# One block for an attention layer and a mixture of experts, with the experts' first operands made in the last attention chunks

## The reference

```python
# attention, per sequence of 512 tokens, 16 heads of 32
q, k, v = relu(x @ w_q.T), relu(x @ w_k.T), x @ w_v.T
vk  = einsum('bhen,bhdn->bhed', pad(v, one row of 1.0), k)
out = einsum('bhed,bhdn->bhen', vk, q)
out = out[:, :, :-1] / (out[:, :, -1:] + 1e-15)
x   = layernorm(x + out @ w_proj.T + b_proj)
# experts: 8, router by sigmoid of logits, golden zone, top-2 fallback
w    = router_weights(x @ Wr)
mid  = silu(x @ Wg[e] (+ LoRA)) * (x @ Wu[e] (+ LoRA))
x    = layernorm(x + sum_e w[:, e] * (mid @ Wd[e] (+ LoRA)))
```

## Time and profile before

| | us |
|---|---|
| median of 3 runs | 2446.73 |
| lowest and highest | 2446.03, 2448.91 |
| the profiled execution's own time | 2444.87 |
| its span | 2443.1 |
| mean granted TensorE clock, share of full | 0.976 |

### The profile page before, as it was taken

The page is one execution under the profiler, slowest core; times in us unless marked ns, Lnnn a source line. Parts: engine busy times, 40 slices in busy tenths (PEclk is TensorE's granted clock), DMA queues, the critical chain, the costliest instruction groups (busy, mean ns, idle before and its releaser), DMA issues. The chain is left out here.

```text
span 2443.1 us, 30851 instructions
## 1 busy us (share of the span) xinstructions
PE 2303.7 (94%) x10684; PEld 1868.2 (76%) x10684; DVE 1605.9 (66%) x2393; ACT 853.1 (35%) x1375; POOL 697.3 (29%) x499
## 2 busy tenths in 40 slices
PE   8897999999979999997999689999999999999997
PEld 6786788888857888885888468777777778888885
DVE  5556676777757956675344786667667886666665
ACT  4444222222214322222222254333344434444442
POOL 0002333444421222220000433224323543333331
PEclk9998999999989999998999999999999999999999
DMA  5654222222223001000000121222111121111110
GB/s 198 217 151 154 61 69 69 69 69 69 72 72 146 18 18 35 1 1 22 1 0 1 44 78 52 78 93 76 39 52 52 52 87 52 52 52 52 52 35 35
DMA packets 91010, 155.34 MB, mean 64 GB/s; under 512 B 6288, under 2 KB 55440, under 8 KB 84256
## 3 DMA queue, kind: packets, MB, share of 16 engines
q1 hardware_dynamic: 90912, 154.07, 18.8%
HBM read 114.20 MB, written 39.85 MB: 63 GB/s over the span
## 5 line engine op out<-in xcount | busy, mean ns | idle before, releaser
L1497 PE MATMUL moe_pu<-moe_b_hi,moe_a_hi 128*128 128x512 f32 x896 | 352.6, 394 | 25.3 <-ACT moe_c_last L1888 9.3
L1498 PE MATMUL moe_pu<-moe_b_lo,moe_a_hi 128*128 128x512 f32 x896 | 350.7, 391 | 0.0
L1499 PE MATMUL moe_pu<-moe_b_hi,moe_a_lo 128*128 128x512 f32 x896 | 350.5, 391 | 0.0
L2057 DVE TENSOR_TENSOR moe_a_lo<-moe_up_raw,moe_a_hi 128x512 fp32r<-128x512 f32 x192 | 185.6, 982 | 147.5 <-ACT moe_a_hi L1764 147.4
L1421 DVE SCALAR_TENSOR_TENSOR acc<-ffn_pd,ffn_wts,acc 128x512 f32<-128x512 f32 x256 | 177.8, 748 | 88.8 <-PE ffn_pd L101 88.6
L2089 DVE SCALAR_TENSOR_TENSOR acc<-moe_ring,moe_wts,acc 128x512 f32<-128x512 f32 x256 | 190.6, 746 | 63.0 <-PE moe_ring L1499 59.1
L1722 POOL TENSOR_TENSOR moe_h_lo<-moe_c_t,moe_h_hi 128x512 fp32r<-128x512 f32 x96 | 128.9, 1344 | 342.6 <-ACT moe_h_hi L1764 342.6
L1497 PEld LDWEIGHTS moe_pu<-moe_b_hi,moe_a_hi 128*128 128x128 f32 x896 | 169.4, 189 | 67.0 <-issue 24.5
L1497 PE MATMUL moe_ring<-moe_dn_hi,moe_h_hi 128*128 128x512 f32 x512 | 203.4, 397 | 6.4 <-DVE acc L2089 3.5
L1498 PE MATMUL moe_ring<-moe_dn_lo,moe_h_hi 128*128 128x512 f32 x512 | 200.2, 391 | 0.0
L1499 PE MATMUL moe_ring<-moe_dn_hi,moe_h_lo 128*128 128x512 f32 x512 | 199.9, 390 | 0.0
(11 more groups left out here) (403 smaller groups left out, 5263.5 us busy)
## 6 DMA issues: line engine op xcount, KB each, us to landing
moe_up_raw<-in_e_up SPq DMA_DIRECT2D x28, 1024.0 KB, 5.8
moe_dn_raw<-in_e_dn SPq DMA_DIRECT2D x28, 512.0 KB, 3.6
xh<-in_out_hi SPq DMA_DIRECT2D x32, 256.0 KB, 2.6
zs<-in_out_z SPq DMA_DIRECT2D x32, 256.0 KB, 3.2
xl<-in_out_lo SPq DMA_DIRECT2D x32, 256.0 KB, 3.4
ssd_z_raw<-zs SPq DMA_DIRECT2D x16, 512.0 KB, 3.9
in_w_raw<-in_in_w SPq DMA_DIRECT2D x4, 1024.0 KB, 7.7
x<-xh SPq DMA_DIRECT2D x8, 512.0 KB, 4.2
```

Source lines behind the costliest of these rows:

```text
L1497: pe.matmul(out, lh, rh, start=first, stop=False, skip_group_check=True)
L1498: pe.matmul(out, lh, rl, start=False, stop=False, skip_group_check=True)
L1499: return pe.matmul(out, ll, rh, start=False, stop=True, skip_group_check=True)
L2057: tt_(a_lo[:, q], src, raw(a_hi[:, q]), ALU.subtract).then_inc(s_alo, 1)
```

## The change

`attn_phase` is removed and its code moves into the experts' function, now `attn_experts`, with one set of semaphores and no barrier between the layers. Both layers' tiles are placed by hand; an operand of the experts that shares memory with an attention tile waits until that tile is read for the last time. The loops over sequences are written out as 16 chunks. PSUM tiles are shared: X is `pvk`, Y is (`pt`, `pk`), Z is `po`, the ring is (`pv`, `pq`).

- `xt` and ScalarE's copy into it are gone; TensorE transposes x from `acc`.
- GpSimd adds the bias to `acc` (`with_bias`, one 128x512 addition for each chunk), ahead of its part of the norm; VectorE's `norm_in` has one addition where it had two.
- In chunks 8 to 12 TensorE turns the eight chunks of the first half of the tokens (`ahead_x`), ScalarE copies them to `xr`. Chunk 12 makes the logits of parts, chunk 13 the plain logits and their turning.
- After chunks 8 to 11 ScalarE and VectorE cut the weights of q0 to q5 and x for q0 and q1. The first router's parts 0, 1, 2 stand after chunks 13, 14, 15, part 3 in the drain's first round; its comparison uses the second weight buffer as scratch, so the load of slot 1's weights waits for `s_router`.
- The drain's rounds 1 to 3 each make one product of slot 0 (`FIRST`) before `project`, and contain one `x_low` each; two more follow.
- Slot 0 now has the same lists as the others, without `down` and `add_down`.

The core of the diff:

```diff
+            def with_bias(n):
+                pool.wait_ge(s_xT, n + 1)
+                nc.gpsimd.tensor_tensor(acc[:, n], acc[:, n], bias[:], ALU.add).then_inc(s_xb, 1)
...
+            pool.wait_ge(s_bias, 16)
+            for n in range(NCH):
+                with_bias(n)
+                if n >= CPB and n != NCH - 1:
+                    deviation(n - CPB)
+                if n == 2 * CPB - 1:
+                    weight_sums(0, 0, 0, 0)
+                if n == 2 * CPB:
+                    weight_sums(0, 0, 0, 1)
+                    weight_sums(0, 0, 0, 2)
+                if n == PLAIN_AT:
+                    x_sums(0, 0)
+            deviation(NCH - CPB - 1)
             x_sums(0, 1)
+            deviation(NCH - CPB)
             x_sums(0, 2)
+            for m in range(NCH - CPB + 1, NCH):
+                deviation(m)
...
+        AHEAD = {8: (0, 1), 9: (2, 3), 10: (4, 5), 11: (6,), 12: (7,)}
+        PARTS_AT, PLAIN_AT, TOKENS_AT = 12, 13, 13
...
+            def ahead_x(i):
+                ch = sum(AHEAD.values(), ())[i]
+                if i:
+                    pe.wait_ge(s_xr, i)
+                pe.wait_ge(s_ln, ch + 2)
+                for kt in range(KT):
+                    ins = pe.transpose(pt[:, bass.ts(kt, P)], acc[:, ch, bass.ts(kt, P)], ident[:])
+                ins.then_inc(s_et, 1)
...
@@ ScalarE @@
+            for n in range(NCH):
+                chunk(n)
+                if n == 8:
+                    up_high(0, 0, 0, 0)
+                    up_high(0, 0, 0, 1)
...
+                if n == 13:
+                    router_functions(0, 0)
+                if n == 14:
+                    router_functions(0, 1)
...
@@ TensorE, drain round c @@
+                if c:
+                    ring.enter(0)
+                    up(0, *FIRST[c - 1])
+                pe.wait_ge(s_pa, m if c else m + 1)
+                project(m, (pv, pq)[c % 2])
@@ VectorE, after chunk n @@
+                if n == 13:
+                    dve.wait_ge(s_lgt, 1)
+                    router(0, 0)
+                if n == 14:
+                    router(0, 1)
+                if n == 15:
+                    router(0, 2)
+            for c in range(CPB):
+                m = NCH - CPB + c
+                divide(m)
+                if c:
+                    norm_out(m - 2)
+                low_out(m)
+                norm_in(m - 1, (pv, pq)[(c - 1) % 2] if c else pv)
+                if c == 0:
+                    router(0, 3)
+                if c < 3:
+                    x_low(0, (4, 2, 3)[c])
+            norm_out(NCH - 2)
+            x_low(0, 5)
+            norm_in(NCH - 1, (pv, pq)[(CPB - 1) % 2])
+            x_low(0, 6)
+            norm_out(NCH - 1)
```

More of the change, by code:

```diff
@@ L1830, in slot @@
                 more = not at(n, LAST)
-                plain = more and not at(n, 0, *MERGING)
+                plain = more and not at(n, *MERGING)
                 following = lambda *qs: [up_high(n + 1, 1 - s, u + s, q) for q in qs]
@@ new lines, in add_vk, with attend @@
+            def add_vk(n, c):
+                pe.wait_ge(s_vr, n + 1)
+                for g in range(G):
+                    bank = pvk[:, g // 2, (g % 2) * 256:(g % 2) * 256 + VW]
+                    ins = pe.matmul(bank, kk[:, bass.ts(g, P)], vo[:, g], start=(c == 0 and g % 2 == 0),
+                                    stop=(c == CPB - 1), skip_group_check=True)
+                ins.then_inc(s_vk, 1)
+            def attend(m):
+                pe.wait_ge(s_od, m + 1)
+                for g in range(G):
+                    ins = pe.matmul(po[:, g // 2, (g % 2) * 256:(g % 2) * 256 + OW], qT[:, m % CPB, g], bd[:, g],
+                                    start=True, stop=True)
+                ins.then_inc(s_o, 1)
@@ new lines, in turn_out, with project @@
+            def turn_out(m):
+                pe.wait_ge(s_od, m + 1 + 1)
+                for kt in range(KT):
+                    ins = pe.transpose(pk[:, bass.ts(kt, P)], o[:, kt].rearrange("p h d -> p (h d)"), ident[:])
+                ins.then_inc(s_oT, 1)
+            def project(m, bank):
+                pe.wait_ge(s_olo, m + 1 + 1)
+                for kt in range(KT):
+                    ins = product(pe, bank[:], (o_hi[:, kt], o_lo[:, kt]), (wp_hi[:, kt], wp_lo[:, kt]),
+                                  kt == 0, kt == KT - 1)
+                ins.then_inc(s_p, 1)
@@ new lines, in _ @@
+            turn_x(0)
+            for n in range(NCH):
+                chunk(n)
+            pe.wait_ge(s_bd, NB)
+            pe.wait_ge(s_qTc, NCH)
+            attend(NCH - CPB)
+            for c in range(CPB):
+                m = NCH - CPB + c
+                pe.wait_ge(s_olo, m + 1)
+                turn_out(m)
+                if c < CPB - 1:
+                    attend(m + 1)
+                if c:
[3 more added lines that the diff above has]
+                project(m, (pv, pq)[c % 2])
@@ new lines, in norm_out, with divide @@
+            def norm_out(m):
+                dve.wait_ge(s_arstd, m + 1)
+                ts(acc[:, m], rr[:], amv[:, 0:1], arstd[:], ALU.subtract, ALU.mult).then_inc(s_ln, 1)
+            def divide(m):
+                division.round(m)
+                dve.wait_ge(s_o, m + 1)
+                outs = po[:].rearrange("p t (g n) -> p (t g) n", g=2)
+                division.link(ts(den[:], outs[:, :, P:OW], AEPS, None, ALU.add))
+                division.link(nc.vector.reciprocal(den[:], den[:]))
+                dve.wait_ge(s_oT, m + 1)
+                for g in range(G):
+                    ins = tt_(o[:, g], outs[:, g, 0:P].rearrange("p (h d) -> p h d", h=HG),
+                              den[:, g].unsqueeze(2).broadcast_to([P, HG, AD]), ALU.mult)
+                ins.then_inc(s_od, 1)
@@ L2048, in _ @@
+            chain = Chain(dve, c_router, 0)
             link = chain.link
```

877 lines of the change are left out of this document (404 added, 473 removed).

## The result

| | us |
|---|---|
| median before, 11 runs | 2447.62 (2444.55 to 2448.99) |
| median after, 11 runs | 2441.82 (2438.55 to 2445.11) |
| ratio of the two, 95% interval | 0.9982 (0.9974 to 0.9990) |
| forecast | 2433, from 2422 to 2442 |

What follows compares the result with a forecast made beforehand. TensorE, busy 94% of the span, bounds the kernel, so only its standing time can be gained: -20.9 - 6.2 + 9.6 + 4.0 = -13.5 us, giving 2431.4 in the profile's terms and 2433 for the median, range 2422 to 2442.

Steps and rivals of the forecast that it cites:

- slot 1's -6.2: Slot 1: of 3.67 us idle time and 3.9 of low clock lost before, 1.4 remains, giving -6.2 us.
- TensorE's work moved into the chunks, +9.6: Chunks 8 to 13: turnings, plain logits, logits of parts and their turning cost full length, none hidden, +9.6 us.
- Waits in the chunks, +4.0: Chunks 11, 12, 14, 15: TensorE waits as GpSimd's additions hold up `norm_out` and router parts, taken as +4.0 us.
- The 5.3: Chunks 11, 12, 14, 15: sum of the waits if GpSimd always comes first, in full by the lock rule, 5.3 us.
- Table loads, 0: Chunks, ScalarE: table loads for sigmoid and exp lie in its idle time and cost nothing.
- The drain: After the last chunk: TensorE stands 5.9 us, rounds take 6.5, router part 3 4.9, turnings at T = 14.4, 20.9, 27.4.
- Slot 0: First expert slot: q4 starts at 43.1 after 4 us standing; slot 1 starts at T = 56.5, was 77.4: -20.9 us.
- (a): Chunks, drain, slot 0: waits don't come, the drain's 5.9 and slot 0's 4 us half filled; about 2424, chance 0.2.
- (b): Drain: longer, five `x_low` and norms held up by `x_sums`, gives back 8 to 10 us; about 2442, chance 0.17.
- (c): Chunks 8 to 15: lock rule in full strength makes `turn_out` wait; +22 us, 2455, slower; chance 0.08.
- (d): Slot 1's weights: their load waits for the router, so the change does not overlap; 2446, chance 0.03.

Runs made afterwards that it cites:

- g1: Changed kernel with 1248 bytes of its small tiles placed ahead of `xr`, bringing `a_lo` to 640 modulo 2048: 2429.71 us against 2446.13, 0.9933.
- h2: g1's kernel with router part 2 in chunk 15, part 3 before the drain's first division, early products one round earlier: 2425.95 us, 0.9911.
- e3: Kernel before with 32 bytes of padding before `a_lo` and 32 behind it: 2459.86 us, 1.0052.
- e4: Kernel before with 32 bytes of padding before `b_lo` and 32 behind it, every tile behind moving by 64 bytes: 2462.47 us, 1.0059.
- f3: Kernel before with pads of 64 bytes around `a_lo`: 2457.03 us, 1.0042.
- f4: Kernel before with pads of 64 bytes around `b_lo`: 2460.12 us, 1.0054.
- g2: Kernel before with 128 bytes ahead of `a_lo`, everything behind moving along: 2461.48 us, 1.0063.
- h4: Kernel before with both `b_hi` and `b_lo` 128 bytes off, `a_hi` and `a_lo` in step with the rest: 2460.54 us against 2445.76, 1.0056.
- e1: Changed kernel with 32 bytes of padding before `xr`, moving `xr`, raw up weights and `a_lo` to a multiple of 64: 2436.29 us against 2446.68, 0.9958.
- e2: Changed kernel with 32 bytes of padding behind the raw up weights, moving only `a_lo` and small tiles behind it: 2438.05 us, 0.9963.
- f1: Changed kernel with three small tiles (96 bytes) placed before `xr`, putting `a_lo` on a multiple of 128: 2435.56 us against 2445.81, 0.9958.
- h3: Kernel before with 128 bytes ahead of `h_hi` and `h_lo`, the down products' weights: 2452.69 us, 1.0029.

## Why the prediction was wrong

**The step that failed** is one that the sum leaves out: its last term is slot 1's -6.2, and the matmuls of all slots are taken at the pace that they had before. The change also placed every tile of the experts, and I put the new addresses at nothing without saying so; of the later slots the sum only says that written-out loops cost nothing. From slot 1 to the end of the span were 1021.3 us, the forecast makes it 1015.1, and 1028.7 were measured. With `a_lo` at the old distance modulo 256 (g1) they are 1014.9. So 13.8 us were lost there to 32 bytes, 12.1 by the medians of the two kernels. The slower groups alone make 17 of it (15 and 2); a part of that is taken back by shorter waits, which from slot 1 on are 16.4 us in all where g1 has 18.5.

With the bytes repaired the profiled execution is 13.3 us faster than the one before, and 13.5 were forecast; by the medians it is 16.4 (2429.7 where 2433 was forecast). That the first pair is so close is partly luck, since single executions of one kernel differ by more, and since two of the terms below miss in opposite directions.

Point by point, by its own steps:

- **TensorE's work moved into the chunks, +9.6**: the stretch shows +12.8, less 2.3 of waits, so 10.5. Right in mechanism, 0.9 too small. With the waits below, 1.7 too large, the two misses nearly cancel: 13.6 forecast, 12.8 measured.
- **Waits in the chunks, +4.0**: 2.3. The waits before the turnings in chunks 11 and 12 came at 0.69 and 0.68 (1.2 each forecast), the one at `turn_q` of chunk 14 at 0.96 (2.0), that of chunk 15 not at all (0.9). GpSimd was first, as the order of the lists said, but `norm_out` ended at t = 4.4, not 4.9 (1277.82 + 1.49, with t = 0 at 1274.9): I had added a whole scaling, 0.55, behind GpSimd's addition, and it ends 0.29 behind it. The Trainium skill's rule of the lock (SBUF — State Buffer, "Who interferes with whom") says that between GpSimd and a VectorE instruction in a two-port mode, which `tensor_scalar` can enter, whoever issues first holds the shared ports for its whole instruction. The trace agrees: thirteen of the scalings end 0.28 or 0.29 us after GpSimd's instruction does. The 5.3 that I drew from it did not follow, since it took these ends too late, and since in chunk 15 `turn_q` found q ready.
- **Table loads, 0**: right. ScalarE's timeline after, with the two loads of the chunks and the functions that need them, is shown behind this list. They are issued 9.9 and 8.9 us ahead of their functions, in idle time.
- **The drain**: router part 3 took 4.9 us (1364.33 to 1369.22), as said; turnings at T = 14.1, 21.9 and 28.0 (14.4, 20.9 and 27.4); the wait 5.39 (5.9).
- **Slot 0**: q4 at 43.9 (43.1), its wait 3.69 (4), slot 1 at 56.9 (56.5). Right. h2 bears out that VectorE's list set the pace, as argued: with 3 us less of it there the stretch is 2.9 us shorter, though TensorE's early products were moved in the same run.
- **Slot 1, -6.2**: no wait of the kind that stood at 1441.65 is left, and the 35 us from its start on (1414.7 to 1450) are granted 1.00 both here and in g1, so the low clock that I kept a part of is gone; in g1 all of the time from slot 1 to the end is 6.4 shorter.
- **Rivals**: none of the four was it. The waits of (a) did come. The result lies near (b), but the drain was not longer. (c) is refuted as a price: no wait at `turn_out` in any chunk. As for (d), from slot 1 on the profile lists no wait of TensorE for a load.

ScalarE's rows, sigmoid in chunk 14 and exp in chunk 15:

```profile
1324.23 1.28 ACT L1995 ACT_TABLE_LOAD   x1
1334.08 0.26 ACT L1995 ACTIVATE moe_pr<-moe_lg 128x64 f32<-128x64 f32 x1 [8.57 <-DVE moe_lg L2553]
...
1339.86 1.28 ACT L1998 ACT_TABLE_LOAD   x1
1348.72 0.26 ACT L1998 ACTIVATE moe_sel<-moe_lg 128x64 f32<-128x64 f32 x1 [7.58 <-DVE moe_lg L2561]
```

## What to carry to other kernels

When an edit moves tiles, compare the number of matmuls in a window without waits before asking which wait has changed: 443 against 435 in 100 us, at full clock and 100% busy, is a loss that no idle time shows. In products like these, keep the tiles that TensorE streams and those it loads as weights at the same remainder modulo 256 bytes of a partition, and pad them so, rather than packing to 32 bytes. And work on the bounding engine that is moved into a stretch where that engine is busy anyway saves nothing; what this change gained is idle time and low clock, while 10 us of TensorE's own work went along at full price.

## What the runs showed of the hardware that was not expected

A group of three matmuls (128x128 weights, 512 columns, fp32r) takes 0.681 us when streams and weights lie at equal remainders modulo 256, and 0.692 to 0.700 when its own don't: 32, 64 and 128 bytes off all cost, 256 and 512 don't, and shifting all tiles together by 64 doesn't. The granted clock is 1.00 in all these windows.

The pairwise rule isn't whole. In e3, e4, f3, f4, g2 and h4 the down products' four tiles agreed among themselves and only stood apart from `b_hi`, and their group still rose to 0.687 to 0.696; in the changed kernel, e1 and e2 they had not moved against `b_hi` at all and it rose to 0.685 or 0.686 (not in f1, 0.6808); in h3 the up group rose a little (0.6844) though only `h_hi` and `h_lo` had moved. Much of this lies where TensorE changes from one kind of product to the other. In the changed kernel, e1, e2, e3, e4 and h4 after an up product the first five down matmuls start 0.229 to 0.231 us apart on the mean, and from the sixth on it is 0.227, as before. In h3 the first up matmul after a down product and the last one before the next take 0.232 to the next start, those between 0.227. In f4 and g2 the down matmuls from the sixth on are slow too (0.231), which that does not explain. Why one pair's placement counts for another's, and why it is 256 bytes, stays open.
